# A perceiver block on one core: both output projections in three passes of rounded halves, feed forward weights turned in the tail, tail buffers laid out anew

## What is computed

```python
x = x + xattn(layernorm(x), ctx, ctx, Wq, Wk, Wv, Wo)   # x [16,32,512], ctx [16,512,512]
x = x + attn(layernorm(x), Wq2, Wk2, Wv2, Wo2)          # rope, causal mask, 32 positions
x = x + (einsum('bsi,oi->bso', layernorm(x), w) + bias) # w [512,512] from 3 bit codes
# both attentions: 32 query heads, 8 key/value heads, head size 16, softmax, and last: out @ Wo
# w = (q / 7) * (2 * n) - n, q the unpacked codes, n one number per 32 of them
```

## Time and profile before

| | |
|---|---|
| median of 3 runs (lowest to highest) | 361.53 us (359.78 to 364.54) |
| profiled execution: its own time | 360.37 us |
| its span, first to last instruction | 358.5 us |
| mean granted TensorE clock | 0.990 |
| busy: PE, DVE, ACT, POOL | 337.7, 229.9, 192.7, 104.5 us |
| DMA, mean over the span | 115 GB/s |

### The profile page before, as it was taken

How to read it: one execution, slowest core, us unless ns; L and a number is a source line. 1 busy time by engine, 2 the same in 40 slices (tenths; PEclk the granted TensorE clock), 3 DMA queues, 4 the chain that set the end, 5 groups by cost and what they waited for, 6 DMA issues and landing times.

```text
span 358.5 us, 8376 instructions
## 1 busy us (share of the span) xinstructions
PE 337.7 (94%) x2958; PEld 244.7 (68%) x2962; DVE 229.9 (64%) x402; ACT 192.7 (54%) x369; POOL 104.5 (29%) x196
## 2 busy tenths in 40 slices
PE   7999778999999999999999999998798989999996
PEld 4755546777777777777777777775456748875664
DVE  2977655766766766758667657667846237886652
ACT  4643224667767666776677676658446421253320
POOL 1431813133133132240331331322103141651420
PEclk9999898999999999999999999999999999999999
DMA  7980497575776485875867876969400000000002
GB/s 279 398 100 4 95 222 178 142 119 169 159 118 171 81 201 162 131 152 144 118 174 160 110 202 156 166 173 136 58 0 2 2 0 2 1 2 0 2 29 88
DMA packets 35821, 41.25 MB, mean 115 GB/s; under 512 B 15137, under 2 KB 30497, under 8 KB 33697
## 3 DMA queue, kind: packets, MB, share of 16 engines
q1 hardware_dynamic: 35360, 40.74, 52.2%
q10 hardware_dynamic: 432, 0.13, 0.2%
HBM read 24.07 MB, written 1.05 MB: 70 GB/s over the span
## 4 chain that ended last, share of the span: by engine, by line
PE 79%; DVE 8%; DMA 4%; ACT 3%; SPq 2%; issue 2%; POOL 2%; ACTq 0%; DVEq 0%
PE b_c L1087 8%; PE b_d L1028 8%; PE b_s L1049 8%; PE b_v L1003 4%; PE b_c L1232 4%; PE b_v L1005 4%; PE b_v L1004 4%; PE b_k L1005 4%; PE b_k L1003 4%; PE b_k L1004 4%; PE b_x L975 3%; PE b_t L975 3%; DMA kstack<-kparts 2%; PE b_c L1113 2%; PE b_v L1054 2%
## 5 line engine op out<-in xcount | busy, mean ns | idle before, releaser
L769 DVE TENSOR_REDUCE negmax<-b_s 128x1 f32<-128x512 f32 x128 | 88.0, 688 | 68.7 <-PE b_s L1049 61.4
L573 ACT ACTIVATE region<-b_c 128x512 f32<-128x512 f32 x128 | 74.6, 597 | 57.5 <-PE b_c L1087 35.2
L1049 PE MATMUL b_s<-kstack,qstack 96*128 96x512 bf16 x128 | 49.9, 390 | 9.5 <-DVE negmax L769 5.5
L1087 PE MATMUL b_c<-qstack,kstack 108*128 108x128 bf16 x512 | 50.7, 222 | 0.1
L1087 PEld LDWEIGHTS b_c<-qstack,kstack 108*128 108x128 bf16 x512 | 32.8, 99 | 26.3 <-issue 21.4
L471 POOL TENSOR_TENSOR mwide<-negmax,zeros 128x4 bf16<-128x4 f32 x32 | 6.6, 206 | 121.0 <-DVE negmax L769 121.0
L1003 PE MATMUL b_v<-cT_h,wkv_h 128*128 128x512 f32 x64 | 31.7, 495 | 0.0
L1028 PE MATMUL b_d<-region,vaug 128*17 128x128 f32 x1024 | 31.1, 273 | 0.0
L1003 PE MATMUL b_k<-cT_h,wkv_h 128*128 128x512 f32 x64 | 30.7, 480 | 0.0
L462 POOL TENSOR_TENSOR kparts<-kres,zeros 128x512 bf16<-128x512 f32 x16 | 18.9, 1182 | 38.4 <-DVE kres L754 38.4
L1028 PEld LDWEIGHTS b_d<-region,vaug 128*17 128x17 f32 x1024 | 26.6, 98 | 1.7
(11 more groups left out here) (390 smaller groups left out, 680.8 us busy)
## 6 DMA issues: line engine op xcount, KB each, us to landing
cx<-in_ctx_dram SPq DMA_DIRECT2D x16, 1024.0 KB, 4.9
kstack<-kparts SPq DMA_DIRECT2D x96, 128.0 KB, 4.4
qstack<-region SPq DMA_DIRECT2D x76, 32.0 KB, 2.9
xs<-in_x_dram SPq DMA_DIRECT2D x1, 1024.0 KB, 7.8
region<-in_L_xattn_Wq_dram SPq DMA_DIRECT2D x1, 1024.0 KB, 10.0
cx<-in_L_xattn_Wo_dram SPq DMA_DIRECT2D x8, 128.0 KB, 5.1
cx<-in_L_attn_Wq_dram SPq DMA_DIRECT2D x1, 1024.0 KB, 5.4
region<-in_L_attn_Wo_dram SPq DMA_DIRECT2D x8, 128.0 KB, 7.2
```

The lines of the kernel that those rows point to most:

```text
L573: nc.scalar.activation(pT[:, g], b_c[g % 2][:].rearrange("p (a n) -> p a n", a=KT), ACT.Exp, scale=SCALE).then_inc(exp_ready, 1)
L769: nc.vector.tensor_reduce(negmax[:, n % 2, g:g + 1], b_s[:], AX, ALU.max, negate=True).then_inc(max_ready, 1)
L1049: nc.tensor.matmul(b_s[:], qstack[0:STACK, g, n % 4], kstack[0:STACK, n % 4, g], start=True, stop=True).then_inc(s_ready, 1)
L1087: last = nc.tensor.matmul(b_c[g % 2][:, P * a:P * a + P], kstack[0:ROWS, m % 4, g, P * a:P * a + P], qstack[0:ROWS, g, m % 4], start=True, ...
```

## The change

- First output projection: `oT` becomes `oT_h` and `oT_l`. In every slot from n = 2 on ACT writes `oT_h`, now at g = 5, and DVE then writes `oT_l` (`attended_low`); that, no longer ACT's copy, raises `oT_ready`. `wo` is loaded in the opening, into a buffer of its own, split by ACT in slot 0 and by POOL in slot 1 (`low_residual_weights`). Each tile takes 12 matmuls of rounded operands where it took four float32 ones (eight records in the profile).
- Second output projection: the same with `o2T_h`, `o2T_l` (a DVE part of step 19) and `swo_h`, `swo_l`, which ACT and POOL make in a new step 25 `split_output`, four entries of `LATE`.
- Feed forward weights: the turning leaves slots 14 and 15 and becomes step 24 `turn_weights`, four entries of `LATE`, through the two banks of tile 0; `spread_values` of tile 0 waits for all four and stands later in the list, as does `scores` of tile 0.
- Buffers: `wT_h` and `wT_l` hold the halves of `wo` until then, `swq_h` and `swq_l` those of `swo` after the queries; `swkv`, `xn`, `rotq_b`, `k_rot`, `v2`, `swo` and `o2T` move, so `wnat` stays whole into the tail.

```diff
+STEPS += [("turn_weights", 0), ("split_output", 0)]
-LATE = [(0, 3), (1, 3), (2, 3), (3, 3), (6, 2), (7, 2), (8, 2), (4, 3), (9, 2), (10, 2), (5, 3), (11, 2), (12, 2),
-        (15, 0), (6, 3), (13, 2), (16, 0), (7, 3), (8, 3), (9, 3), (10, 3), (11, 3), (14, 2), (12, 3), (13, 3),
-        (15, 1), (17, 0), (16, 1), (14, 3), (15, 2), (17, 1), (18, 0), (16, 2), (15, 3), (19, 0), (18, 1), (17, 2),
+LATE = [(0, 3), (1, 3), (2, 3), (3, 3), (6, 2), (7, 2), (24, 0), (8, 2), (4, 3), (9, 2), (24, 1), (10, 2), (5, 3),
+        (11, 2), (24, 2), (12, 2), (6, 3), (24, 3), (13, 2), (15, 0), (7, 3), (16, 0), (8, 3), (9, 3), (10, 3), (25, 0),
+        (11, 3), (14, 2), (25, 1), (12, 3), (13, 3), (25, 2), (15, 1), (25, 3), (17, 0), (16, 1), (14, 3), (15, 2), (17, 1), (18, 0), (16, 2), (15, 3), (19, 0), (18, 1), (17, 2),
...
-        swq_h, swq_l, wT_h, wT_l = (sb(name, [P, C, D], F32R) for name in ("swq_h", "swq_l", "wT_h", "wT_l"))
+        swq_h, swq_l, wT_h = (sb(name, [P, C, D], F32R) for name in ("swq_h", "swq_l", "wT_h"))
+        with nc.sbuf_tensor("wo_raw", [P, R, D], F32) as plain:
+            wo = plain[:]
+        wT_l = sb("wT_l", [P, C, D], F32R)
+        wo_h, wo_l, swo_h, swo_l = wT_h, wT_l, swq_h, swq_l
...
-        oT = sb("oT", [P, TILES, R, P])
+        oT_h = sb("oT_h", [P, TILES, R, P], F32R)
+        with nc.sbuf_tensor("region", [P, 11264], F32) as plain:
+            region = plain[:]
+        rounded = sb("region_r", [P, 11264], F32R)
+        oT_l = rounded[:, 4096:6144].rearrange("p (t r n) -> p t r n", t=TILES, r=R)
...
-        swkv, swo = region[:, 4096:5120], region[:, 5120:7168]
-        swkv = swkv.rearrange("p (i c n) -> p i c n", i=2, c=C)
-        swo = swo.rearrange("p (r n) -> p r n", r=R)
+        swkv = wkv_raw
+        swo = region[:, 6144:8192].rearrange("p (r n) -> p r n", r=R)
-        xn = by_tile(region[:, 7168:9216])
-        rotq_b = region[:, 9216:10240].rearrange("p (i n) -> p i n", i=2)
-        k_rot = by_tile(region[:, 10240:10752])
-        v2 = by_tile(region[:, 10752:11264])
+        rotq_b = region[:, 8192:9216].rearrange("p (i n) -> p i n", i=2)
+        old_kparts = kparts[:].rearrange("p i k n -> p (i k n)").bitcast(F32)
+        k_rot = by_tile(old_kparts[:, 0:512])
+        v2 = by_tile(old_kparts[:, 512:1024])
-        wo = old_cx[:, 0:2048].rearrange("p (r n) -> p r n", r=R)
+        xn = by_tile(old_cx[:, 0:2048])
-        o2T = q_rot.rearrange("p t (r b n) -> p t r b n", r=R, b=BPT)
+        o2T_h, o2T_l = (o.rearrange("p t r (b n) -> p t r b n", b=BPT) for o in (oT_h[:], oT_l))
...
-        def weight_chunk(n, g):
-            if n == B - 2 and g in (2, 4, 6):
-                return g // 2 - 1
-            return C - 1 if (n, g) == (B - 1, 0) else None
...
+                for g in range(G):
+                    sp.dma_start(wo[HD * g:HD * g + HD],
+                                 xwo_d[R * HD * g:R * HD * (g + 1)].rearrange("(r d) n -> d r n", r=R)).then_inc(weights_loaded, 16)
...
-                    sp.wait_ge(ctx_transposed, C * (B - 1))
-                    for g in range(G):
-                        sp.dma_start(wo[HD * g:HD * g + HD],
-                                     xwo_d[R * HD * g:R * HD * (g + 1)].rearrange("(r d) n -> d r n", r=R)).then_inc(weights_loaded, 16)
...
+            def low_residual_weights():
+                for r in range(R):
+                    pool.wait_ge(wo_high, r + 1)
+                    nc.gpsimd.tensor_tensor(wo_l[:, r], wo[:, r], wo_h[:, r].bitcast(F32), ALU.subtract).then_inc(wo_ready, 1)
+            def split_output(r):
+                pool.wait_ge(swo_high, r + 1)
+                nc.gpsimd.tensor_tensor(swo_l[:, r], swo[:, r], swo_h[:, r].bitcast(F32), ALU.subtract).then_inc(swo_ready, 1)
...
+                if not looped(trip) and n == 1:
+                    low_residual_weights()
...
-                    if g == 6 and live(n - 2, trip):
-                        m = n - 2
-                        wait(act, o_transposed, 1, m, 1, trip)
-                        tile = m // BPT + trip
-                        nc.scalar.activation(oT[:, tile, :, S * (m % BPT):S * (m % BPT) + S],
-                                             o_cols.rearrange("p (r t) -> p r t", r=R), ACT.Copy).then_inc(oT_ready, 1)
...
-                    c = weight_chunk(n, g)
-                    if c is not None:
-                        act.wait_ge(w_transposed, c + 1)
-                        nc.scalar.activation(wT_h[:, c], b_tx[c % 2][:], ACT.Copy).then_inc(wT_high, 1)
...
+                    if not looped(trip) and n == 0 and g % 2 == 1:
+                        act.wait_ge(weights_loaded, 16 * G)
+                        nc.scalar.activation(wo_h[:, g // 2], wo[:, g // 2], ACT.Copy).then_inc(wo_high, 1)
+                    if g == 5 and live(n - 2, trip):
+                        m = n - 2
+                        wait(act, o_transposed, 1, m, 1, trip)
+                        tile = m // BPT + trip
+                        nc.scalar.activation(oT_h[:, tile, :, S * (m % BPT):S * (m % BPT) + S],
+                                             o_cols.rearrange("p (r t) -> p r t", r=R), ACT.Copy).then_inc(oT_high, 1)
...
-                nc.scalar.activation(o2T[:, t].rearrange("p r b t -> p b r t"),
-                                     bank_x[t][:].rearrange("p (b r t) -> p b r t", b=BPT, r=R), ACT.Copy).then_inc(o2T_ready, 1)
+                nc.scalar.activation(o2T_h[:, t].rearrange("p r b t -> p b r t"),
+                                     bank_x[t][:].rearrange("p (b r t) -> p b r t", b=BPT, r=R), ACT.Copy).then_inc(o2T_high, 1)
+            def turn_weights(c):
+                act.wait_ge(w_transposed, c + 1)
+                nc.scalar.activation(wT_h[:, c], (bank_x, bank_y)[c % 2][0][:], ACT.Copy).then_inc(wT_high, 1)
+            def split_output(r):
+                act.wait_ge(sq_summed, TILES)
+                act.wait_ge(tail_weights_loaded, 16 * G)
+                nc.scalar.activation(swo_h[:, r], swo[:, r], ACT.Copy).then_inc(swo_high, 1)
...
+            def attended_low(m, trip):
+                wait(dve, oT_high, 1, m, 1, trip)
+                at = (slice(None), m // BPT + trip, slice(None), slice(S * (m % BPT), S * (m % BPT) + S))
+                nc.vector.tensor_tensor(oT_l[at], o_cols.rearrange("p (r t) -> p r t", r=R), oT_h[at].bitcast(F32),
+                                        ALU.subtract).then_inc(oT_ready, 1)
...
+                    if g == 5 and live(n - 2, trip):
+                        attended_low(n - 2, trip)
...
-                    c = weight_chunk(n, g)
-                    if c is not None:
-                        dve.wait_ge(wT_high, c + 1)
-                        nc.vector.tensor_tensor(wT_l[:, c], b_tx[c % 2][:], wT_h[:, c].bitcast(F32), ALU.subtract).then_inc(wT_ready, 1)
...
-                    dve.wait_ge(w_transposed, C)
-                    dve.wait_ge(qstack_loaded[(B - 1) % 4], 16 * SLOTS * (B // 4 - 1))
+                    dve.wait_ge(ctx_transposed, C * (B - 1))
...
+                if t == 0:
+                    dve.wait_ge(qstack_loaded[(B - 1) % 4], 16 * SLOTS * (B // 4 - 1))
...
+                if t == 0:
+                    for i in range(4):
+                        dve.wait_ge(kstack_loaded[i], 16 * SLOTS * B // 4)
...
+            def attend(t):
+                dve.wait_ge(o2T_high, t + 1)
+                nc.vector.tensor_tensor(o2T_l[:, t].rearrange("p r b t -> p b r t"),
+                                        bank_x[t][:].rearrange("p (b r t) -> p b r t", b=BPT, r=R),
+                                        o2T_h[:, t].rearrange("p r b t -> p b r t").bitcast(F32), ALU.subtract).then_inc(o2T_ready, 1)
+            def turn_weights(c):
+                dve.wait_ge(wT_high, c + 1)
+                nc.vector.tensor_tensor(wT_l[:, c], (bank_x, bank_y)[c % 2][0][:], wT_h[:, c].bitcast(F32), ALU.subtract).then_inc(wT_ready, 1)
...
-            def weight_part(c, t):
-                if t == 0:
-                    pe.wait_ge(w_ready, 1)
-                    pe.wait_ge(ctx_low, C * B)
-                    count(pe, wT_ready, c - 1)
-                at = D * t + P * c
-                piece = nc.tensor.transpose(b_tx[c % 2][:, P * t:P * t + P], wnat[:, at:at + P], ident[:])
-                if t == TILES - 1:
-                    piece.then_inc(w_transposed, 1)
...
-                        if n == B - 2:
-                            weight_part(g // 2, 2 * (g % 2) + second)
...
-                    pe.wait_ge(weights_loaded, 16 * G)
-                for semaphore, value in ((k_res, B), (wT_ready, C), (exp_ready, G * B))[t:t + 1]:
+                    pe.wait_ge(wo_ready, R)
+                for semaphore, value in ((k_res, B), (ctx_low, C * B), (exp_ready, G * B))[t:t + 1]:
                     pe.wait_ge(semaphore, value)
-                last = nc.tensor.matmul(bank_x[t][:], oT[:, t, r], wo[:, r], start=(r == 0), stop=(r == R - 1))
-                if r == R - 1:
```

(36 more changed lines are left out.)

5 lines of the change are left out of this document (2 added, 3 removed).

## The result

The changed kernel takes 369.67 us (median of 4 runs, 368.99 to 370.42) beside 361.09 us of the kernel before on the same chip: 1.0223 times as long, 95% interval 1.0147 to 1.0299. I had forecast 366.0. It is slower; whether by more than 2% the interval leaves open. Ratios and intervals leave out runs that lie more than 1.5% above the fastest of their kernel. The profiled execution took 370.18 us with a span of 368.4; before, 360.37 and 358.5.

What follows compares the result with a forecast made beforehand. PE was taken as full from 60 to 237 us, with DVE nearly full from 296 to 320. The tail's 7.15 us lag less a 3.2 us earlier start gave +4.0, the clock +1.6: 360.4 to 366.0 us, range 359.5 to 371.

Steps and rivals of the forecast that it cites:

- rival B: Tail: the same lag as forecast, but the clock stays up, 364.4 us; chance 0.22.
- rival C: Steady slots: the PE, ACT, DVE chain holds back DVE's next maximum, 0.3 to 0.5 us a slot, 371 us; chance 0.15.
- a case that had 0.23: Whole kernel: slower by more than 2%, above 368.8 us; chance 0.23.
- Slots 14 and 15, -1.9: Slots 14 and 15: losing the turning takes 2.1 us off the chain, against 0.3 for `attended_low`, 1.9 us net.
- 262 to 285 us, 0: Slot 15 and tile 1's projection: 0.5 us for `attended_low` and about the same saved by tile 1 cancel, 0.
- tile 3, -0.8: Tile 3's first projection: twelve rounded matmuls instead of four float32 ones save 0.8 us.
- The tail's first half: From tile 3's projection to `spread_values` of tile 0: DVE's new entries and PE's transposes make it 3.8 us late.
- POOL's queue: Tail: four `swo` subtractions ahead of step 17 of tile 0 make step 18 of tile 0 start 8.9 us late.
- The clock in the tail: Behind PE's gap of over 3 us ahead of step 18 of tile 0: half clock, +1.6 us.
- The tail's second half: From step 18 of tile 1 on: 8.0 us late there, `o2T_l` waits against second-projection savings, 7.15 us at the end.
- Opening and steady slots, 0: `wo` loads, copies and subtractions are hidden in the opening and slots 0 and 1; steady slots keep 0.2 us slack: 0.
- Rival D: Tail: it absorbs the new steps and the projections' savings hold, 355 to 358 us; chance 0.18.

Runs made afterwards that it cites:

- before_free: The kernel before without the turning of the feed forward weights (it uses the query weights' halves): 359.13 us, ratio 0.9942.
- early_pool: Changed kernel, `swo` quarters split as tile 3's chunks finish, turned chunks copied once, halved later on ACT and POOL: 364.81 us; with 16 matmuls on zeros (`early_pool_warm`) 361.86.
- warm_gaps: The changed kernel with 29 matmuls on zeros put into PE's idle stretches: 366.84 us, ratio 1.0104.
- passes_alone: `late_turn` with 11 matmuls on zeros ahead of the tail and without the turning (query weights' halves used instead): 358.92 us, ratio 0.9938.
- late_turn: `early_pool` with tile 0's spreading ahead of tile 3's queries again and the turns behind tile 3's scores: 363.58 us, ratio 1.0082.
- no_turn: The changed kernel without the turning (feed forward uses the halves of the first projection's weights): 367.85 us, ratio 1.0139.

## Why the prediction was right and wrong

The forecast was 3.7 us low. The range held, but by luck: 369.67 is above the 361 to 369 that the forecast's own mechanism and its rival B were given, and only rival C, which did not happen, carried the range on to 371. It is also above 368.8, a case that had 0.23. The mechanism of the tail was right; the step that failed is the sum's "Its start is earlier by 1.9 (slots 14, 15), 0 (262 to 285), 0.5 (tile 2, less the 0.3) and 0.8 (tile 3): 3.2 us". It measured 0.4. A second term was too small, in the tail: 10.2 us late where 7.15 and 1.6 for the clock were summed.

- **Slots 14 and 15, -1.9.** Right: `before_free` gives 2.1 us, and the scores that end slot 15 start at 269.98 instead of 271.99, 2.0 us earlier.
- **262 to 285 us, 0, and tile 3, -0.8.** Both terms left out the clock. By the chain tile 2's projection starts at 283.73 instead of 284.69, 0.96 us early where 2.0 had been won. `early_pool`, whose clock is full there, shows what took the rest. In its timeline the same scores start at 269.67:

```profile
269.67 0.39 PE L1084 MATMUL b_s<-kstack,qstack 96*128 96x512 bf16 x1 [1.63 <-DVE negmax L806]
```

and its chain has the projections of tiles 2 and 3 so:

```profile
282.41 3.01 PE b_c L1141 x12
289.50 3.05 PE b_x L1141 x12
```

From those scores to tile 2's projection it takes 12.74 us (12.71 in `warm_gaps`), the changed kernel 13.75 at the lower clock: 1.0 us. Tile 3's group took 4.61 us instead of 3.05: 1.6 us. The projections themselves save less than I put down, 3.65 and 3.70 to 3.01 and 3.05, that is 0.65 each and not 0.8. With 0.3 for the two, 1.0 and 1.6 make up the missing 2.8 of 3.2. And with the clock held the forecast start comes: in `passes_alone`, which does the same work up to there and stands at the maximum above as the kernel before does (228.64 against 228.61), the tail starts at 292.79, 3.0 us before 295.83. I had expected a fall only behind the longest gap.
- **The tail's first half.** `xnT_l` began at +5.65 and ended at +6.3 (forecast +6.6), `spread_values` ended at +10.4 (+10.1). Of this lag 2 us are the new order alone: in `late_turn` the spreading starts 4.06 us behind the tail's start, in `no_turn`, new order and no turning, 6.06. I had booked it under DVE and ACT.
- **POOL's queue.** L502 of tile 3 at +16.6 (forecast +16.1, though 11.9 in the earlier trace rows and the lag of 3.8 make 15.7), L521 of tile 0 ending at +27.0 (+26.7), no gap between them, PE idle for 3.1 us: as said.
- **The clock in the tail.** +1.6 forecast behind that gap; `warm_gaps` shortens the tail by 1.43, and by 4.0 with the way to it. The Trainium skill's page "TensorE: Matmul & The Clock Gate", "Part 1: The HAM clock gate", has idling bring the array to half rate: the trace agrees, at 0.00 of 2 us and 0.52 behind. Nearer to the two falls that I missed is its section "A second HAM failure mode: psum-queue depth-cycling", where frequent short idling between groups of matmuls makes the clock go back and forth; I had not weighed it. The falls behind idling of 1.63 us and of 0.83, 0.40 and 0.56 us fit it; that it is the cause no run here shows.
- **Step 18 of tile 1.** +33.6, forecast 31.5 and the clock, 33.1.
- **The tail's second half.** From there the lag should have fallen from 9.6 to 8.75 us (7.15 and the clock). It is 10.2 at step 18 of tile 1 and still 10.2 at the end. The mis-sized term is tile 1's 0.25 for `o2T_l`. DVE takes it (336.69) ahead of the scores of tile 3 and has waited 1.08 us for ACT's rounded copy, so the whole wait lies in the chain: 1.2 us.
- **Opening and steady slots, 0.** Right. In the timeline of the SP queue the eight `wo` loads are issued long before the queries are:

```profile
20.87 4.79 SPq L384 DMA_DIRECT2D wo_raw<-in_L_xattn_Wo_dram  x8
34.16 1.88 SPq L321 DMA_DIRECT2D qstack<-region  x3
```

and in the timeline of a steady slot it is 1.81 us from the second turning to the scores of g = 7, against 1.79 in the earlier trace rows:

```profile
149.97 0.27 PE L1104 MATMUL b_d<-ident_sb,o_sb 128*128 128x128 f32 x1
...
150.83 0.29 DVE L774 TENSOR_TENSOR region_r<-b_d,oT_h 128x128 f32 x1 [0.58 <-ACT oT_h L624]
...
151.78 0.39 PE L1078 MATMUL b_s<-kstack,qstack 96*128 96x512 bf16 x1
```

Rival C falls with that. Rival D is half alive in `passes_alone`: the tail can cover the new steps of the passes if they are placed for it, but that kernel leaves the turning out, and what it gives is the 2 us of the freed slots, nothing from the passes. Rival B, the clock staying up, is what `warm_gaps` makes: 366.84, where B had 364.4.

## What to carry to other kernels

A shorter matmul pays only where TensorE ends the stretch, and its operands' halves are work for the other engines: with everything placed well, eight projections in three passes won nothing here. Work that is moved into a stretch with a written-out order costs by the queue that it joins and by what it stands ahead of (3.4 us for four subtractions of 1.28 us on GpSimd, a clock fall included), so move it with a finer semaphore into that engine's idle time. When a change thins out TensorE's work ahead of a dense part, price each thin stretch at the lower clock, not only the longest gap.

## What the runs showed that I had not expected

The clock fell behind much less idling than the 3.1 us gap that I had looked at. Before tile 3's projection PE had idled for 0.83, 0.40 and 0.56 us with transposes between; at 269 us the fall came behind one gap of 1.63 us. And it is not settled by the gap: 0.37 us busy in 268 to 270 was followed by 0.72 and 0.50 in the changed kernel and by 1.00 in `early_pool`. That run had a fall of its own earlier: its clock is at 0.56 from 248 to 250 us and at 0.50 to 254, where the changed kernel has 1.00, and `early_pool_warm` shows the same, since no fill lies there. `early_pool` spreads over 361.4 to 367.0 us in 10 runs and, with 16 fills, over 360.2 to 362.8. That the clock makes this spread is not shown: its mean is 0.981 both at 361.4 and at 367.0 us. What decides whether a thin stretch is followed by a fall was not tried.
